# Sixteen-head attention and a mixture of experts on one core: preparing the weights inside the projections, and the border to attention

## The reference

```python
x = x + layernorm(attn(layernorm(x)))          # x: 4 x 2048 x 256, float32
x = x + layernorm(ffn(layernorm(x)))

def attn(x):                                   # 16 heads of 16
    q, k, v = (x @ w_q.T), (x @ w_k.T), (x @ w_v.T)
    scores = q @ k.T / sqrt(16), with a mask: causal, the first 196 positions see each other
    return softmax(scores) @ v @ w_o.T + b_o

def ffn(x):                                    # 8 experts, the best 2 for each token, and a shared one
    h = swiglu((x @ w1.T + b1) * (x @ w3.T + b3))
    return sum(weight * (h @ w2.T + b2))
```

## Time and profile before

| what | us |
|---|---|
| median of 3 timed runs | 2323.17 (2321.58 to 2323.96) |
| span of the profiled execution, its own time | 2336.2 |
| TensorE busy in it | 2127.6 (91%) |
| ACT busy | 1723.4 (74%) |
| DVE busy | 1547.4 (66%) |
| POOL busy | 704.2 (30%) |
| mean granted clock of TensorE | 0.958 |

### The profile page before, as it was taken

How to read it: one execution, slowest core, us unless ns; L and a number is a source line. 1 busy time by engine, 2 the same in 40 slices (tenths; PEclk the granted TensorE clock), 3 DMA queues, 4 the chain that set the end, 5 groups by cost and what they waited for, 6 DMA issues and landing times. The chain is left out here.

```text
span 2336.2 us, 38360 instructions
## 1 busy us (share of the span) xinstructions
PE 2127.6 (91%) x14197; PEld 1305.7 (56%) x14197; DVE 1547.4 (66%) x2336; ACT 1723.4 (74%) x2176; POOL 704.2 (30%) x652
## 2 busy tenths in 40 slices
PE   5995999999999999999997884999999999999980
PEld 4783333333333333333334883788888888888860
DVE  4663255555555555555555976566899999999975
ACT  4664999999999999999995772333566666666645
POOL 1111000000000000000001443777066666666647
PEclk9997999999999999999999986899999999999995
DMA  5886655555544444555502873444487666766656
GB/s 183 308 291 189 133 94 103 103 102 101 103 66 89 89 87 91 95 103 74 83 10 74 266 234 123 161 153 157 171 245 175 174 174 174 174 174 174 174 162 259
DMA packets 166460, 344.30 MB, mean 147 GB/s; under 512 B 17992, under 2 KB 95432, under 8 KB 158984
## 3 DMA queue, kind: packets, MB, share of 16 engines
q1 hardware_dynamic: 132012, 286.37, 45.7%
q0 software_dynamic: 31952, 47.73, 11.4%
q10 hardware_dynamic: 2316, 7.80, 1.0%
HBM read 196.24 MB, written 145.46 MB: 146 GB/s over the span
## 5 line engine op out<-in xcount | busy, mean ns | idle before, releaser
L1079 ACT ACTIVATE att_prob<-att_scores 128x1024 f32<-128x1024 f32 (+2 forms) x1122 | 997.6, 1035 | 58.9 <-PE att_scores L1025 56.5
L1044 PE MATMUL att_out<-att_prob,att_va 128*32 128x512 f32 (+3 forms) x5000 | 576.9, 542 | 12.9 <-DVE att_prob L1111 12.9
L1025 PEld LDWEIGHTS att_scores<-att_qs,att_ks 50*128 50x128 f32 x2560 | 211.0, 185 | 492.9 <-ACT att_prob L1079 418.3
L1025 PE MATMUL att_scores<-att_qs,att_ks 50*128 50x512 f32 (+3 forms) x2560 | 465.8, 430 | 21.0 <-DMA att_qs<-guard 17.0
L1709 POOL DMA_INDIRECT sums<-moe_y,moe_token x156 | 345.8, 2217 | 240.1 <-ACT moe_y L1963 204.5
L1850 PE MATMUL moe_ps<-moe_xt_hi,moe_w_hi 128*128 128x512 f32 x880 | 352.6, 401 | 2.9 <-ACT moe_h L1936 2.2
L973 POOL DMA_DIRECT2D ctx_scr<-att_cout x64 | 55.1, 861 | 983.7 <-DVE att_cout L1161 944.7
L1850 PE MATMUL moe_ps<-moe_xt_hi,moe_w_lo 128*128 128x512 f32 x880 | 348.3, 396 | 0.3
L1850 PE MATMUL moe_ps<-moe_xt_lo,moe_w_hi 128*128 128x512 f32 x880 | 345.6, 393 | 0.8 <-issue 0.8
L1111 DVE SCALAR_TENSOR_TENSOR att_prob<-att_prob,att_tri 128x512 f32<-128x512 f32 x224 | 144.7, 687 | 269.2 <-ACT att_prob L1079 269.2
L1936 ACT ACTIVATE moe_h<-moe_ps,moe_wb 128x512 f32<-128x512 f32 x220 | 148.5, 677 | 136.9 <-PE moe_ps L1850 93.7
(11 more groups left out here) (242 smaller groups left out, 3238.0 us busy)
## 6 DMA issues: line engine op xcount, KB each, us to landing
qk_parts<-proj_qk SPq DMA_DIRECT2D x64, 512.0 KB
keep_first_weights<-w_experts SPq DMA_DIRECT2D x22, 1412.0 KB, 6.5
moe_wraw<-w_experts SPq DMA_DIRECT2D x21, 1412.0 KB
att_qs<-qk_parts SPq DMA_DIRECT2D x180, 128.0 KB
att_ks<-qk_parts SPq DMA_DIRECT2D x180, 128.0 KB
rows_in<-att_zeros SPq DMA_DIRECT2D x13, 1632.0 KB, 21.4
moe_rows<-rows_in SPq DMA_DIRECT2D x29, 544.0 KB
proj_xin<-x SPq DMA_DIRECT2D x16, 512.0 KB, 3.9
```

The source lines that it names most:

```text
L1025: last = nc.tensor.matmul(pss[e % SBUFS][:, h, at:at + CH - q0], ks[s][rows, half, kt * P:(kt + 1) * P], qs[s][rows, half, c * CH + q0:(c ...
L1044: last = nc.tensor.matmul(pso[k % 2][strip, q0:], va[team % 2][:, kt, strip], probs_of(u)[:, h, at:at + CH - q0], start=(kt == 0), stop=(i ...
L1079: nc.scalar.activation(probs_of(u)[:, half * 2:half * 2 + 2, start:], pss[e % SBUFS][:, :, start:], ACT.Exp, scale=HD ** -0.5)\
```

## The change

`prepare` is gone as a block of its own. Its work stands in `project`'s block: SP issues the first x, then the three weights for queries, keys and values, the next two x, the fourth weight and the gate's. ACT cuts three weights before it normalizes the first chunk, and the fourth behind the first `hi` of x. DVE cuts the first three behind the statistics of chunk 0, the fourth behind those of chunk 1. POOL makes its constants first and issues the zeros of `guard` behind its last step of the stage; it waits for them at the end. TensorE has waits for the constants and for the three lo parts.

At the border to attention SP doesn't wait for the stores at the end of `project`. `qk_stored` and `v_stored` belong to an outer phase now. In `find_maxima`'s first block SP and ACT wait for the stores of chunk 0 only, issue the first loads, and then SP waits for all stores. The ones are written by POOL from its own queue, four DMAs behind the memset and ahead of the masks of the branch. ACT issues the two loads of the guard rows at the end of the second block, behind the branch, and not at the start of attention's block. Buffers are allocated in another order, so that what is loaded early does not lie on what is still being stored.

The diff, cut to its core (the constants that POOL makes are moved unchanged):

```diff
-            prepare(nc, ident, power, minus_one, heads_of, wqkv, wo, gw, w_attn, w_gate, guard)
-            project(nc, ident, power, minus_one, heads_of, norms, wqkv, x_ch, qk_parts, v_scr)
+            qk_stored, v_stored = weights.sem2("qk_stored"), weights.sem2("v_stored")
+            project(nc, ident, power, minus_one, heads_of, norms, wqkv, wo, gw, w_attn, w_gate, guard, x_ch,
+                    qk_parts, v_scr, qk_stored, v_stored)
...
-def prepare(nc, ident, power, minus_one, heads_of, wqkv, wo, gw, w_attn, w_gate, guard):
...
+def project(nc, ident, power, minus_one, heads_of, norms, wqkv, wo, gw, w_attn, w_gate, guard, x_ch, qk_parts, v_scr,
+            qk_stored, v_stored):
...
-        xin = ph.sb2("xin", [P, TPC, D])
+        made = ph.sem("constants_made")
+        iz = ph.sem("identity_zeroed")
+        loaded = [ph.sem(f"weight{m}_loaded") for m in range(5)]
+        cut_hi, cut_lo = ph.sem("weights_hi"), ph.sem("weights_lo")
+        zeroed = ph.sem("scratch_zeroed")
+        qk = ph.sb2("qk", [P, 2, 4, CH], F32R)
+        square = ph.sb("square", [P, 4, CH], BF16)
+        va = ph.sb2("va", [P, TEAMS, TPC, TEAM * HD])
...
-        qk = ph.sb2("qk", [P, 2, 4, CH], F32R)
-        square = ph.sb("square", [P, 4, CH], BF16)
-        va = ph.sb2("va", [P, TEAMS, TPC, TEAM * HD])
+        xin = ph.sb2("xin", [P, TPC, D])
+        raw = ph.sb("raw", [P, 4, KT, D])
+        zeros = ph.sb("zeros", [P, SEQ // 2])
+        parts = [(raw[:, m], [wqkv[h][:, :, m * D:(m + 1) * D] for h in range(2)]) for m in range(3)]
+        parts += [(raw[:, 3], [wo[h][:] for h in range(2)])]
...
-        qk_stored, v_stored = ph.sem2("qk_stored"), ph.sem2("v_stored")
...
+                def load_weights(which):
+                    for m in which:
+                        sp.dma_start(raw[:, m], w_attn[m]).then_inc(loaded[m], 16)
+
                 def step(at):
                     n, s = at(0)
                     if not at(-1):
                         load(0, 0)
+                        load_weights(range(3))
                         load(0, 1)
                         load(1, 0)
+                        load_weights(range(3, 4))
+                        sp.dma_start(gw[:], w_gate).then_inc(loaded[4], 16)
                     if at(3):
...
                 in_steps(sp, NCH, step)
-                for s in range(2):
-                    sp.wait_ge(qk_stored[s], NCH // 2 * 64)
-                    sp.wait_ge(v_stored[s], NCH // 2 * 16)
+                sp.wait_ge(loaded[4], 16)
 
             @block.gpsimd
             def _(pool):
+                nc.gpsimd.memset(ident[:], 0.0).then_inc(iz, 1)
...
+                pool.wait_ge(made, 4)
+
+                def zero_guard():
+                    rows = B * H
+                    pool.dma_start(guard.rearrange("b q h g (i t) -> (b q h) (g i) t", i=2),
+                                   bcast(zeros[0:rows, :], 1, [rows, 2 * GUARD, SEQ // 2])).then_inc(zeroed, 16)
+
                 def step(n, s, nxt, prv):
                     inverse_roots(nc, pool, power, s, mv, std, rstd, mv_done, mv_seen, std_done, rstd_done, n)
                     offsets(nc, pool, minus_one, s, mv, negated, rstd, shift, negated_done, rstd_done, shift_done, n)
+                    if nxt is None:
+                        zero_guard()
 
                 in_pairs(pool, NCH, step)
+                pool.wait_ge(zeroed, 16)
...
                     if prv is None:
+                        pe.wait_ge(made, 4)
+                        pe.wait_ge(iz, 5)
                         turn(0, 0)
+                        pe.wait_ge(cut_lo, 3)
                     pe.wait_ge(lo_done[s], n + 1)
...
+                def cut_weights(which):
+                    for m in which:
+                        whole, cut = parts[m]
+                        act.wait_ge(loaded[m], 16)
+                        nc.scalar.activation(cut[0], whole, ACT.Copy).then_inc(cut_hi, 1)
+
                 def step(n, s, nxt, prv):
                     if prv is None:
+                        cut_weights(range(3))
                         normalize(0, 0)
                         hi(0, 0)
+                        cut_weights(range(3, 4))
                     if nxt is not None:
                         normalize(*nxt)
                     act.wait_ge(qk_stored[s], n * 64)
...
+                def cut_weights(which):
+                    for m in which:
+                        whole, cut = parts[m]
+                        dve.wait_ge(cut_hi, m + 1)
+                        V.tensor_tensor(cut[1], whole, cut[0].bitcast(F32), ALU.subtract).then_inc(cut_lo, 1)
+
                 def step(n, s, nxt, prv):
                     if prv is None:
                         measure(0, 0)
+                        cut_weights(range(3))
                         lo(0, 0)
                         measure(0, 1)
+                        cut_weights(range(3, 4))
                     if prv is not None:
                         bound(*prv)
...
                             head(b, team, h, b * H + team * TEAM + h)
                 if eng is nc.scalar:
                     eng.wait_ge(stored, HEADS * 16 * GUARD + 1)
+            if eng is nc.scalar:
+                load_first_guard(eng)
...
             @block.sync
             def _(sp):
+                sp.wait_ge(qk_stored[0], 64)
+                sp.wait_ge(v_stored[0], 16)
                 load_queries(sp)
+                for s in range(2):
+                    sp.wait_ge(qk_stored[s], NCH // 2 * 64)
+                    sp.wait_ge(v_stored[s], NCH // 2 * 16)
 
             @block.scalar
             def _(act):
+                act.wait_ge(qk_stored[0], 64)
                 load_keys(act)
 
             @block.gpsimd
             def _(pool):
-                fill_ones(pool)
+                load_ones(pool)
...
+        va = ph.sb2("va", [P, SEQ // P, TEAM * VA_W])
+        prob = [ph.sb(f"prob{i}", [P, TEAM, CH]) for i in range(PBUFS)]
+        frac = ph.sb2("frac", [P, 2, CH])
+        poly = ph.sb2("poly", [P, 2, CH])
...
-        def load_ones(sp):
-            sp.wait_ge(ones_made, 1)
+        def load_ones(pool):
+            nc.gpsimd.memset(ones[:], 1.0).then_inc(ones_made, 1)
+            pool.wait_ge(ones_made, 1)
             for s in range(2):
                 for h in range(2):
                     to = h * STRIP + SROWS
-                    sp.dma_start(ks[s][to:to + GUARD].bitcast(F32).rearrange("r g (c t) -> r (g c) t", t=CH),
-                                 bcast(ones[:], 1, [GUARD, HALVES * BCH, CH])).then_inc(ones_set, 16)
+                    pool.dma_start(ks[s][to:to + GUARD].bitcast(F32).rearrange("r g (c t) -> r (g c) t", t=CH),
+                                   bcast(ones[:], 1, [GUARD, HALVES * BCH, CH])).then_inc(ones_set, 16)
 
         def load_queries(sp):
             load_parts(sp, 0, slice(0, 1), first[0], 0)
             load_values(sp, 0, slice(0, 1), first[0])
-            load_ones(sp)
 
         def load_keys(act):
             load_parts(act, 0, slice(0, 1), first[0], 1)
 
-        def fill_ones(pool):
-            nc.gpsimd.memset(ones[:], 1.0).then_inc(ones_made, 1)
-
-        find_maxima(nc, ident, norms, qk_parts, guard, load_queries, load_keys, fill_ones)
-
-        va = ph.sb2("va", [P, SEQ // P, TEAM * VA_W])
-        prob = [ph.sb(f"prob{i}", [P, TEAM, CH]) for i in range(PBUFS)]
+        def load_guard(eng, team):
+            s, b = team % 2, team // TEAMS
+            rows = guard[b, team % TEAMS].rearrange("(g h) r t -> h r g t", g=HALVES)
+            for h in range(2):
+                to = h * STRIP + SROWS
+                eng.dma_start(qs[s][to:to + GUARD].bitcast(F32), rows[h]).then_inc(loaded[s], 16)
+
+        def load_first_guard(act):
+            load_guard(act, 0)
+
+        find_maxima(nc, ident, norms, qk_parts, guard, qk_stored, v_stored, load_queries, load_keys, load_ones,
+                    load_first_guard)
+
         late_prob = ph.sb("late_prob", [P, TEAM, CH])
...
 
             @block.scalar
             def _(act):
-                load_guard(act, 0)
                 for u in RING_UNITS:
```

84 lines of the change are left out of this document (19 added, 65 removed).

## The result

The change took 2315.43 us in the median (2313.28 to 2318.62, 8 runs) against 2322.38 of the kernel before on the same chip: ratio 0.9966, 95% interval 0.9956 to 0.9976. By the ratio that is 7.9 us less (the two medians alone are 7.0 apart). The forecast was 17.8 less. On two more occasions the ratio was 0.9962 and 0.9964, so about 8.4 us.

What follows compares the result with a forecast made beforehand. TensorE was taken to bound the projections, with two holes, start and border, where every engine stands in one chain. 11.1 + 3.3 + 1.4 + 2.0 = 17.8 us off 2323.2 gave 2305.4 us, range 2301.5 to 2311.0.

Steps and rivals of the forecast that it cites:

- start: Before TensorE's first product: with x issued first, that product comes at 15.6 instead of 26.75 us, 11.1 us less.
- stores: End of the projections: SP no longer waits for the last stores, so the next block starts 3.3 us earlier.
- ones: First block of find_maxima: POOL writes the ones and ends at 5.9 us against SP's 7.3, 1.4 us less.
- guard rows' load: Start of attention: loads issued earlier bring a gain between 0.8 and 2.4 us, taken as 2.0.
- none of the stage's own waits depends on those: End of the projections: the guard zeros' 1 MB shares the DMA with the last stores, at no cost to the stage.
- + 0.1: First block of find_maxima: last term of POOL's 5.9 us sum, behind the masks and selects, 0.1 us.
- The ones' landing isn't wanted until attention starts: Border: the landing of POOL's writes of ones is needed only 11 us on.
- POOL ends the block: Rival, chance 0.12: at the border POOL's four writes take 3.23 us each; gain falls to 7.9, time 2315.3 us.
- the 11 that were named: Attention: sign that TensorE's clock rises no more than 11 us behind the first scores.
- the slower rival: Rival, chance 0.03: in attention TensorE's clock stays low; 20 more units at that level give 2336.8 us.
- No instruction of the loops, the attention or the experts is changed: Stages behind the border: their instructions stay as they were; no term in the sum was given for them.
- if anything behind 240 us takes longer than before: Sign, for everything behind 240 us: the forecast is wrong if any of it takes longer than before.

Runs made afterwards that it cites:

- e_start: The change with the store waits back at the projections' end, ones back on SP, guard rows' load back in attention's block; ratio 0.9978 to the kernel before.
- e_wait_back: The change, but SP waits for the stores at the end of the projections again; ratio 0.9976 to the kernel before.
- c_before: The kernel before, unchanged, run again for a second profile; ratio 1.0001 to the kernel before.
- c_after2: The changed kernel, unchanged, run again for a third profile; ratio 0.9964 to the kernel before.
- c_after: The changed kernel, unchanged, run again for a second profile; ratio 0.9962 to the kernel before.
- e_border: Only the border part of the change, with prepare kept as a block of its own; ratio 1.0002 to the kernel before.
- e_ones_sp: The change, but SP writes the ones behind its loads, as before; ratio 0.9955 to the kernel before.

## Why the prediction was wrong

Against five profiles of before (one with other addresses, one with the transposes) (unit 3 at 221.8 to 223.9, mean 223.1) and three of the change (210.5 to 211.8, mean 211.3), by the forecast's steps:

| step | forecast | measured |
|---|---|---|
| start | 11.1 | 10.4 at the first product, 10.7 at the norms |
| stores | 3.3 | 2.9 |
| ones | 1.4 | -3.5 (block 13.2 before, 16.8 now) |
| guard rows' load | 2.0 | 1.8 |
| behind unit 3 | 0 | about -3.4 |
| sum | 17.8 | about 8.4 |

- **The start was right.** x's landing, the hidden cuts and the length of the stage came as written. The 0.7 us between 15.6 and 16.34 are POOL beside DVE and small scatter, which the forecast left out.
- **The stores were right in size**: the block begins 1.5 us behind the norms instead of 4.4. That the zeros of `guard` cost nothing ("none of the stage's own waits depends on those", the last stores) was true only because the wait had been moved. Where it is kept (e_start, e_wait_back) those zeros cost 2.1 to 2.3 us; so the two halves of the change need each other, and the moved wait is worth 4.9 in the changed kernel (216.66 against 211.81).
- **The ones are the step that failed.** Behind the masks the sum for POOL had "+ 0.1", without a row, up to the end of the block. In its place stands the drain, which lasts until the four writes have landed: 6.3 us behind the masks in the change, and 6.4 to 7.7 us in itself over the profiles. The forecast priced the issues, where it expected any danger, and these were cheaper than thought (0.57 us against 0.75). "The ones' landing isn't wanted until attention starts" was right for TensorE, but POOL itself waits for it before the block can end. Of the rivals, "POOL ends the block" had the right engine and, at 2315.3, nearly the time, but not the mechanism: it needed writes of 3.23 us each. The time agrees only because the loss behind unit 3 was added to a smaller one here. No row of before shows a drain with POOL's writes under way: every earlier direct write of POOL's was either waited for inside its block or far from the block's end. One row of before could have warned that such a drain can be long, though (source view of L1676 in before):

```profile
L1676 POOLq DRAIN  x1: 6724/6724/6724, 2327.3 to 2327.3; - x1
```

  This is at the end of the program. POOL's last instruction there ends at 2330.4, the drain at 2334.1, and its last write had been issued at 2257.8, so what it waits for in those 3.7 us isn't known. The range for the drain at the border should have had the landing as its dear end.
- **The guard rows' load was right**, at 1.8 against 2.0, with the second chunk's values as the next to be late, as written: unit 3 waits 1.97 us for `att_vin`. The clock, in the windows of the change (answers to the earlier trace rows):

```profile
207.00:212.00 5.00, 3.03 (x16) 0.70 (x12) 4.54 (x9) 1.91 (x3) 0.00 (x0) 0.50 0.55 150
212.00:217.00 5.00, 4.84 (x40) 1.82 (x36) 0.80 (x2) 3.85 (x5) 0.00 (x0) 0.77 0.56 155
217.00:222.00 5.00, 5.00 (x44) 1.65 (x40) 0.57 (x2) 4.77 (x6) 0.82 (x1) 1.00 0.63 173
```

  A mean of 0.77 between 0.5 and 1 puts the rise at 214.3, 12.1 us behind the first scores (9.5 before), a little more than the 11 that were named. Counted from unit 3 it is 3.8 against 3.2. But this scatters from one execution to the next. The last windows of c_before and of c_after2 in which the clock was still low (length, busy, count; then clock, DMA share, GB/s):

```profile
232.00:237.00 5.00, 5.00 (x34) 0.81 0.94 186
```

```profile
218.00:223.00 5.00, 5.00 (x26) 0.62 0.57 160
```

  They put the rise at 233.9 and 221.8, 16.5 and 18.5 us behind the first scores, and 10 behind unit 3 in both. From unit 3 to the last output (`att_cout`) these two attentions took 1034.1 and 1035.3 us, against 1030.8 in the first profile of before and 1031.3 in that of the change. So what the slower rival describes, a late rise, does come, for some 3 us, but in both kernels.
- **"No instruction of the loops, the attention or the experts is changed" was no reason to count nothing there.** This is the second step that failed: some 3.4 us are lost behind unit 3. The forecast's own sign of being wrong, "if anything behind 240 us takes longer than before", came. In the profiles 1.7 us of it lie in the output projection, whose length goes with TensorE's clock, and 1.3 in attention. Why the change should meet the low clock more often is open.

## What to carry to other kernels

Here a transfer that POOL issued near the end of a block held the block until it had landed, whoever needed it; issue such a one early in a long block, or from SP, whose drain took 0.6 us at most. When a wait is moved, look for what is moved under its old place as well: 1 MB that was put near the end of a stage delayed the stores there, though it had landed before they were issued. A gain at one point of a chain isn't a gain in time until the later stages are seen to take as long as before, and single profiles scatter too much to show 3 us there.

## What the runs showed of the hardware beyond that

- POOL's drain at a block's end: 0.65 us in `find_maxima`'s first block with nothing outstanding (but 6.7 at the program's end, see above), 6.4, 6.8, 7.1, 7.3 and 7.7 us (e_wait_back, the change, c_after, e_border, c_after2) behind four writes of 32 KB.
- POOL's issue of such a write took 0.56 to 0.72 us; SP's of the same write 0.62 to 1.2.
- SP's and ACT's issues of six loads took 2.7 to 2.8 us in e_start, 3.5 to 3.6 with POOL's writes (e_wait_back) or pending stores (e_ones_sp) alone, 3.6 and 4.8 with both (e_border), and 6.9 with both behind the 1 MB of zeros (the change).
- TensorE's clock in the output projection, whose products come in groups with gaps between them, isn't the same in each execution of one program: 113.8 us at a mean clock of 0.96 and 117.1 at 0.91 in two profiles of the kernel before, 114.2 at 0.96 and 117.4 at 0.91 in two of the change.
